# Issuing the attention scores by query and by key one after the other instead of alternating

## What is computed

```python
scores = jnp.einsum('bhqd,bhkd->bhqk', q, k) / jnp.sqrt(jnp.float32(dh))   # dh = 8
attn = jax.nn.softmax(scores, axis=-1)
out = jnp.einsum('bhqk,bhkd->bhqd', attn, v)
```

## Time and profile before

| | |
|---|---|
| median of 3 runs | 2834.36 us |
| profiled execution, its own time | 2836.33 us |
| span of the profiled execution | 2834.1 us |
| busy TensorE | 2400.3 us (85%) |
| busy VectorE | 1536.4 us (54%) |
| busy ScalarE | 1521.5 us (54%) |
| mean granted clock of TensorE | 0.913 |

### The profile page before, as it was taken

How to read it: one execution, slowest core, us unless ns; L and a number is a source line. 1 busy time by engine, 2 the same in 40 slices (tenths; PEclk the granted TensorE clock), 3 DMA queues, 4 the chain that set the end, 5 groups by cost and what they waited for, 6 DMA issues and landing times. The chain is left out here.

```text
span 2834.1 us, 69952 instructions
## 1 busy us (share of the span) xinstructions
PE 2400.3 (85%) x27712; PEld 1672.2 (59%) x27712; DVE 1536.4 (54%) x4449; ACT 1521.5 (54%) x2379; POOL 544.8 (19%) x730
## 2 busy tenths in 40 slices
PE   3656989898989989898989889897989989888975
PEld 2434647575666657575666657574756657564643
DVE  3343555656465565656465665656465565634232
ACT  1324545565665555665656655665555565644432
POOL 2111112121212222121212121121212122111111
PEclk9555989999999999999999999999999999998965
DMA  2100010111010110101010101111010111110000
GB/s 112 34 16 13 22 29 21 31 25 42 23 44 24 28 33 20 32 24 43 23 44 24 43 18 30 26 27 36 23 44 23 37 25 32 24 25 20 14 20 17
DMA packets 103752, 84.21 MB, mean 30 GB/s; under 512 B 15000, under 2 KB 102681, under 8 KB 102937
## 3 DMA queue, kind: packets, MB, share of 16 engines
q1 hardware_dynamic: 103449, 79.91, 11.5%
HBM read 14.21 MB, written 4.19 MB: 6 GB/s over the span
## 5 line engine op out<-in xcount | busy, mean ns | idle before, releaser
L984 DVE TENSOR_REDUCE smax<-by_query_banks 128x8 f32<-128x616 f32 (+1 forms) x512 | 515.9, 1008 | 353.6 <-PE by_query_banks L1303 353.1
L770 ACT ACTIVATE probs<-by_key_banks 77x1024 f32<-77x1024 f32 (+1 forms) x512 | 517.8, 1011 | 216.7 <-PE by_key_banks L1325 213.3
L1240 PEld LDWEIGHTS by_key_banks<-moe_w,hid 128*128 128x128 f32 x4096 | 476.0, 192 | 14.1
L1240 PE MATMUL by_key_banks<-moe_w,hid 128*128 128x128 f32 x4096 | 483.7, 275 | 0.0
L752 ACT ACTIVATE hid<-by_query_banks,cols 128x512 f32<-128x512 f32 x512 | 334.9, 686 | 274.0 <-PE by_query_banks L1231 272.0
L1373 PE MATMUL weighed_bank<-probs,values 128*32 128x128 f32 x8192 | 365.3, 301 | 2.2 <-ACT probs L770 1.6
L1303 PE MATMUL by_query_banks<-k_int,q_int 32*128 32x128 f16 (+1 forms) x4096 | 199.9, 220 | 166.5 <-DVE smax L984 87.3
L1303 PEld LDWEIGHTS by_query_banks<-k_int,q_int 32*128 32x128 f16 x4096 | 121.7, 99 | 334.0 <-issue 220.1
L1373 PEld LDWEIGHTS weighed_bank<-probs,values 128*32 128x32 f32 x8192 | 211.0, 117 | 95.3 <-issue 45.7
L1325 PE MATMUL by_key_banks<-q_int,k_int 32*128 32x128 f16 x4096 | 223.2, 233 | 8.1 <-ACT probs L770 5.3
L765 ACT ACTIVATE m_sb<-turned_bank 16x128 f16<-16x128 f32 x256 | 67.7, 264 | 298.1 <-PE turned_bank L1355 298.1
(11 more groups left out here) (232 smaller groups left out, 3878.5 us busy)
## 6 DMA issues: line engine op xcount, KB each, us to landing
q_int<-q_nat SPq DMA_DIRECT2D x256, 128.0 KB, 2.7
k_int<-k_nat SPq DMA_DIRECT2D x128, 128.0 KB, 2.7
k_int<-k_nat SPq DMA_DIRECT2D x128, 77.0 KB, 2.3
x_tok<-in_x SPq DMA_DIRECT2D x17, 256.0 KB, 3.1
q_int<-m_sb SPq DMA_DIRECT2D x256, 4.0 KB
out<-res SPq DMA_DIRECT2D x16, 256.0 KB, 2.3
ctx_tok<-in_ctx SPq DMA_DIRECT2D x17, 154.0 KB
hid<-in_moe_w SPq DMA_DIRECT2D x1, 2048.0 KB
```

The lines of the kernel that those rows point to most:

```text
L770: act.activation(probs[h % 2][0:nk], by_key[0:nk], ACT.Exp, scale=DH ** -0.5)\
L984: dve.tensor_reduce(smax[h // 2 % 2][:, pair, :], scores, AX.X, ALU.max, negate=True)\
L1240: last = pe.matmul(B[e % 2][:, seq_tok(b)], hidden[e % 2][:, c, seq_tok(b)], moe_w2[:, e, c, :], start=(c == 0), stop=(c == CHUNKS - 1))
```

## The change

The two generators of a step are no longer run in turn. `alone` runs the by-query generator to its end and then the by-key generator. The step now issues: wait for smax, mask by query, eight matmuls by query, wait for probs, mask by key, eight matmuls by key. Steps with only one half are as before.

```diff
-from itertools import zip_longest
...
                         both = [score(m, h)] if here else []
                         both += [turned(*partner)] if partner else []
-                        for _ in zip_longest(*both):
-                            pass
+                        for each in both:
+                            alone(each)
                         continue
```

## The result

| | before | after |
|---|---|---|
| timed runs | 9 | 9 |
| their median, us | 2832.34 | 2844.74 |
| lowest | 2826.18 | 2837.39 |
| the profiled execution | 2836.33 | 2842.01 |
| its span | 2834.1 | 2839.8 |

The changed kernel is slower by 0.42%: ratio 1.0042, interval 1.0026 to 1.0058, which is 7 to 16 us. One of the nine runs of before took 9019.31 us, far from the other eight (2826 to 2840), and hardly moves the median. The forecast was slower too, but by 25 us (2859.4), twice as much as was measured.

The account below looks back on a forecast made before the run. It took attention's score steps, waiting by turns for probs and smax, as the bound. 1.6 us over thirteen full passes (20.8) plus 4 us for partial passes, together 25, gave a median of 2859.4 us, range 2838 to 2888.

Parts of the forecast that it names:

- What bounds it, the list of waits: Attention's score steps wait by turns for ScalarE's probs (135 times) and VectorE's smax (105 and 80 times).
- kind 1: Steps where probs is last and TensorE was idle: by query goes out early, nothing added; about half the steps.
- What sixteen together cost after the change: Partnered score steps: by key begins when by query's last pair has begun, adding 0.20 us at 128 columns, 0.13 at 77.
- kind 2: Steps where TensorE itself comes just in time: 0.3 us a pass at full clock, 0.45 at low, 0.33 last both-mask step.
- kind 3: Steps where smax is last, mostly late in the pass: by key starts 0.20 us later; 0.65 us a pass.
- the 4 us for the partial ones: The 46 partnered steps of the partial passes, many at low clock and smax-last, at 0.09 us each.
- rival C: Instruction issue sets the pace, sixteen take 0.33 us in any order: 0 to 8 us, at most 2843; chance 0.16.
- The both-mask step: Steps masked on both sides: by-key mask now follows by-query scores; last one 0.33 us a pass, 0.15 at 1499.81.
- The gain of parted lanes: Where a smax-last step follows a probs-last one, by query starts early: 0.15 us gained, once a pass.
- rival B: Lanes come apart and win in the wide steps: 1.35 us gained a pass, 18 us in all, 2817; chance 0.11.
- The sum: A full pass: 0.45 + 0.3 + 0.33 + 0.65 - 0.15 = 1.6 us; thirteen full passes 20.8 us.
- Rival D: The low-clock stretch grows by half or goes: 1 us a pass, 13 us in all, either way; chance 0.06.

Follow-up runs that it names:

- e1: the kernel after, but both waits and both masks ahead of the two blocks of eight in every step; 2833.59 us, ratio to before 1.0004.
- e3: e1, with each eight's matmuls sorted so that four on one set of rows follow one another; 2835.80 us, ratio to before 1.0015.
- e2: the kernel after, but waits and masks of both sides first in the three steps a pass with two masks; 2811.92 us, ratio to before 0.9931.
- e7: e2 with four useless matmuls more among the experts of each of 16 groups; 2837.34 us, ratio to before 1.0021.

## Why the prediction was wrong in size

**What bounds it, the list of waits, kind 1: right.** The wait for probs went from by query (70.7 us) to by key, and shrank (16.3).

**What sixteen together cost after the change: wrong, the step that failed.** "After the change the by-key eight begin when the last pair by query has begun." They begin 0.02 us after the first pair. The 0.20 us at 128 columns and 0.13 at 77 are 0.01 to 0.02 in the rows (0.35 against 0.33 us to the next operation, medians of wide steps; 0.35 against 0.34 of narrow ones; 0.56 against 0.55 at the low clock, where 0.22 more was forecast). The prediction had the fact in hand, that different rows overlap, and then let the issue order decide when a row set begins; here the row sets take their work independently of each other. Of the 1.6 us a pass, kind 2 at full and low clock (0.3 + 0.45) and kind 3's unmasked steps (0.65 less the 0.15 of 1499.81) rested on this price: 1.25 us, some 16 us over 13 passes, and most of the 4 us for the partial ones. Measured by e1 it is 0.19 us a pass, 2.5 over 13. This was rival C's result, but not by its mechanism: what e3 shows is not a pace of issue that any order meets, but sets of rows that don't wait for each other.

The Trainium skill, in TensorE: Matmul & The Clock Gate, section "The mechanism", says that matmuls are strictly first in, first out, in start and in end. The trace disagrees for matmuls on different rows: at 1481.80 by key starts before by query's second pair at 1481.84, which was issued ahead of it. The measurement decides. Had the rule held here, the by-key eight could not have begun before the last by-query matmul had started, which is what the forecast charged for.

**The both-mask step: right place, price too small, one place too few.** Estimated were 0.33 us at the last one and 0.15 at the first. Measured, by the marks of after against those of e2 from the first wide score: the first costs 0.02 us that stay (next mask at 32.98 against 32.96: smax starts 0.43 sooner there, 31.16 against 31.59, and takes it back), the second 0.42 (38.77 to 39.21) and the last 0.41 (1.31 to 1.72 us). The second was not priced at all. Together 0.85 us a pass where 0.48 stood. The price is what an eight apart from the other costs: 0.33 us, and what follows the mask starts 0.53 us after it where the second mask started after 0.44.

**The gain of parted lanes: right at the place named.** By key at 4.26 instead of 4.41 us: 0.15, as forecast. The rows show it at further places that the prediction held for blocked (by query at 13.23 instead of 13.51, the first mask at 16.76 instead of 17.28). By the end of the stretch e2 is 0.38 us ahead of e1, where 0.15 a pass was forecast; against before 0.19 is left, since the blocks take the other 0.19. This is rival B's mechanism, at a fraction of its price of 1.35 us a pass.

**The sum.** Blocks 0.19, parted lanes -0.38, masks 0.85: 0.66 us a pass, 8.6 us in 13, where 1.25, -0.15 and 0.48 stood. The 13 passes show 9.4, and the medians 12.4 (7 to 16). The partial passes have such steps as well, about 3 us if each costs as in a full pass; their own change in the profile (776.5 to 772.8 us) is hidden by the clock. Right sign for half the right reason: the term that made up most of the sum was not there, and a term held small made up for a part of it. That the range, 2838 to 2888, holds the measured 2844.74 is luck in part: it reached so low for work absorbed elsewhere and for the clock, not because the blocks might be free.

**Rival D: its size was right.** 13 us either way was allowed for. In the change itself it hardly showed: the low time is 97 and 101 us in the narrow stretches, 7 and 24 in the middle ones, and the same in the last. The low time in the middle is what makes the 11.9 us above more than 8.7. But e2 and e7 differ by 18 us through it.

## What to carry to other kernels

Matmuls on different sets of rows need no interleaving by hand: issue each side when its own wait is over, and here they mixed by themselves, at 0.01 to 0.02 us a step. What separates them is an instruction over the whole array between the two, here 0.42 us at each of two steps (a third hid it); put such instructions ahead of both. Issue first the side whose consumer is free to take it: by key first cost 1.7 us a pass. And where the clock drops in part of each pass, a gain of under one per cent in one kernel's total is to be believed only when windows at an equal clock show it in the stretch that was edited.

## What the runs showed of the hardware that was not expected

- Sixteen matmuls issued in blocks of eight (after), or of four on one set of rows (e3), start by turns, and the next operation starts 0.35 and 0.37 us after the first of them; interleaved in the program 0.33.
- The same narrow stretch of work takes 27.52 us at clock 1.00, 28.84 at 0.88 and 29.87 to 30.21 at 0.83, and which of them a pass gets changes with work that is elsewhere: e7, with some 13 us of padding, takes 25 us more than e2.
- With the masks' matmuls gone the mean granted clock was lower (0.894 and 0.887 against 0.913 and 0.912).
